# A four-layer graph network: TensorE's fp32 transposes of the activations replaced by two 192 KB DMA transposes per tile

## What is computed

```python
h = relu(layernorm(x));  x = x + gat(relu(gat(h, W1, ...)), W2, ...)
h = relu(layernorm(x));  x = x + gcn(relu(gcn(h, W3, b1)), W4, b2)
# gat: h = x @ W; softmax over each node's incoming edges; weighted sum of h[src]; + bias
# gcn: h = x @ W; sum over incoming edges of h[src] * dinv[src] * dinv[dst]; + bias
```

## Time and profile before

| | |
|---|---|
| median of 3 executions | 2389.45 us (2389.22 to 2395.45) |
| span of the profiled execution | 2395.2 us; the page gives no time of it beside its span, and the slowest of the three is 0.25 us above that |
| TensorE (PE) busy | 2277.9 us, 95% of the span |
| VectorE (DVE), ScalarE (ACT), GpSimd (POOL) busy | 67%, 39%, 39% |
| SP's plain DMAs (q1) | 308.94 MB, 36.7% of the 16 DMA engines' time |
| GpSimd's indirect DMAs (q0) | 172.47 MB, 23.2% of it |
| mean granted TensorE clock | 0.978 of full speed |

### The profile page before, as it was taken

How to read it: one execution, slowest core, us unless ns; L and a number is a source line. 1 busy time by engine, 2 the same in 40 slices (tenths; PEclk the granted TensorE clock), 3 DMA queues, 4 the chain that set the end, 5 groups by cost and what they waited for, 6 DMA issues and landing times.

```text
span 2395.2 us, 45199 instructions
## 1 busy us (share of the span) xinstructions
PE 2277.9 (95%) x14017; PEld 1464.0 (61%) x14017; DVE 1607.5 (67%) x3699; ACT 940.8 (39%) x1271; POOL 933.2 (39%) x1469
## 2 busy tenths in 40 slices
PE   5999999999999999999999999999999999999954
PEld 3666666666666666666566666665666666666621
DVE  5788877775577675443699999655556666668732
ACT  2333343333344454334354445333333434333311
POOL 2333324431534442211366565455433333234354
PEclk9999999999999999999999999999999999999966
DMA  4333332225455554343688888776689988777666
GB/s 167 112 115 116 117 108 98 99 93 184 149 188 192 187 189 151 127 157 118 203 273 288 288 285 276 242 229 216 227 264 308 304 301 303 240 239 258 229 216 203
DMA packets 150732, 482.51 MB, mean 201 GB/s; under 512 B 22265, under 2 KB 22344, under 8 KB 150516
## 3 DMA queue, kind: packets, MB, share of 16 engines
q1 hardware_dynamic: 112804, 308.94, 36.7%
q0 software_dynamic: 37840, 172.47, 23.2%
HBM read 262.87 MB, written 225.76 MB: 204 GB/s over the span
## 4 chain that ended last, share of the span: by engine, by line
PE 68%; DVE 11%; issue 8%; DMA 8%; POOL 4%; ACT 1%; DVEq 0%; POOLq 0%; ACTq 0%
PE ps_h L870 56%; PE ps_z L857 7%; DMA row_in<-in_x,idx_b 4%; DVE bn L1046 2%; DVE pre L1042 2%; DMA edge_mem<-rows,idx_d 2%; DVE pre L1040 2%; PE ps_e L888 1%; DMA out<-base_out,idx_o 1%; PE ps_e L941 1%; PE ps_e L942 1%; DVE edge_mem L1104 1%; POOL rstd L566 1%; POOL edge_mem L551 1%; POOL idx_b L617 1%
## 5 line engine op out<-in xcount | busy, mean ns | idle before, releaser
L870 PE MATMUL ps_h<-w_hi,z_hi 128*128 128x384 f16 x3792 | 929.5, 327 | 0.0
L870 PE MATMUL ps_h<-w_lo,z_hi 128*128 128x384 f16 x3792 | 929.1, 327 | 0.0
L870 PE MATMUL ps_h<-w_hi,z_lo 128*128 128x384 f16 x3792 | 928.7, 327 | 0.0
L1079 DVE TENSOR_TENSOR z_lo<-ps_z,z_hi 128x768 f16<-128x768 f32 x316 | 301.8, 955 | 357.9 <-ACT z_hi L778 354.8
L870 PEld LDWEIGHTS ps_h<-w_lo,z_hi 128*128 128x128 f16 x3792 | 372.0, 98 | 247.2 <-issue 3.0
L870 PEld LDWEIGHTS ps_h<-w_hi,z_lo 128*128 128x128 f16 x3792 | 371.9, 98 | 246.9 <-issue 2.7
L870 PEld LDWEIGHTS ps_h<-w_hi,z_hi 128*128 128x128 f16 x3792 | 372.2, 98 | 219.2 <-issue 15.9
L771 ACT ACTIVATE row_out<-ps_h,grow 128x768 f32<-128x768 f32 x237 | 213.1, 899 | 544.0 <-PE ps_h L870 543.7
L857 PE MATMUL ps_z<-ident,z 128*128 128x128 f32 x1896 | 264.8, 277 | 42.4 <-ACT z L789 35.4
L778 ACT ACTIVATE z_hi<-ps_z 128x768 f16<-128x768 f32 x316 | 254.2, 804 | 46.7 <-PE ps_z L857 46.0
L857 PEld LDWEIGHTS ps_z<-ident,z 128*128 128x128 f32 x1896 | 226.5, 143 | 72.5 <-ACT z L789 40.0
(11 more groups left out here) (213 smaller groups left out, 2324.5 us busy)
## 6 DMA issues: line engine op xcount, KB each, us to landing
rows<-row_out SPq DMA_DIRECT2D x316, 384.0 KB, 3.1
row_in<-rows SPq DMA_DIRECT2D x118, 384.0 KB, 4.2
x_rows<-pre SPq DMA_DIRECT2D x79, 384.0 KB, 4.3
row_in<-x_rows SPq DMA_DIRECT2D x79, 384.0 KB, 4.0
row_in<-in_x SPq DMA_DIRECT2D x78, 384.0 KB, 3.1
rows<-e_out SPq DMA_DIRECT2D x60, 384.0 KB, 3.9
w_raw<-in_L_gnn_W SPq DMA_DIRECT2D x4, 2304.0 KB, 10.0
base_rows<-base_out SPq DMA_DIRECT2D x20, 384.5 KB, 4.3
```

The lines of the kernel that those rows point to most:

```text
L870: last = nc.tensor.matmul(ps_h[s][:, a, 0:HALF], zp[s][:, c, :], wp[:, c, a * HALF:(a + 1) * HALF], start=(c == 0 and zp is z_hi and wp is ...
L1079: V.tensor_tensor(pair3(z_lo[t.slot]), psum_pair(ps_z), pair3(z_hi[t.slot]), ALU.subtract).then_inc(z_lo_ready, 1)
```

## The change

It transposes the activations with the DMA engines in place of TensorE, and splits them before the transposition. ScalarE writes each tile twice from the same input: the upper fp16 part into the left half of `z_half` (128 x 1536 in fp16) and then fp32 `z`. VectorE subtracts the one from the other into the right half. SP issues a transposing DMA for the left half when ScalarE has written it, and another for the right half when VectorE has: 192 KB each, into `z_turn`, 128 x 12 x 128 in fp16 with four buffers. The transposes on TensorE, `ps_z` and the copy of it on ScalarE go. Every step ahead of the products comes one window earlier: ScalarE makes `z(t+3)`, VectorE `low_parts(t+2)` and `prepare(t+4)`, SP turns t+2, loads are for t+5. The weight buffers are two pairs in place of three, and layer 4's weights are dealt with in windows 43 to 53 of `3f`.

```diff
-    t = 0 if phase["before"] else -4
+    t = 0 if phase["before"] else -5
...
-        w_hi = [sb(f"w_hi{s}", [P, KC, D], F16) for s in range(3)]
-        w_lo = [sb(f"w_lo{s}", [P, KC, D], F16) for s in range(3)]
+        w_hi = [sb(f"w_hi{s}", [P, KC, D], F16) for s in range(2)]
+        w_lo = [sb(f"w_lo{s}", [P, KC, D], F16) for s in range(2)]
...
+        z_half = [sb(f"z_half{s}", [P, 2 * D], F16) for s in range(2)]
+        z_turn = [sb(f"z_turn{s}", [P, 2 * KC, P], F16) for s in range(4)]
...
+            def turn(t):
+
+                wait(sp, z_ready, t.g + 1)
+                sp.sem_inc(sp_gate, 1)
+                sp.dma_start_transpose(z_turn[t.slot4][:, 0:KC, :], z_half[t.slot][:, 0:D]).then_inc(z_turned[t.slot4], 16)
+                wait(sp, z_lo_ready, t.g + 1)
+                sp.sem_inc(sp_gate, 1)
+                sp.dma_start_transpose(z_turn[t.slot4][:, KC:2 * KC, :], z_half[t.slot][:, D:2 * D]).then_inc(z_low_turned[t.slot4], 16)
...
             def window(t, side, i, r):
-                if t.exists(4) and t.plus(4).phase["name"] in ("3f", "4f"):
-                    load(t.plus(4))
+                if t.exists(5) and t.plus(5).phase["name"] in ("3f", "4f"):
+                    load(t.plus(5))
                 if t.exists(-1):
                     store(t.plus(-1))
+                if t.exists(2):
+                    turn(t.plus(2))
...
-                    nc.scalar.activation(pair3(z_hi[b.slot]), psum_pair(ps_z), ACT.Copy).then_inc(z_hi_ready, 1)
...
+                if t.exists(3):
+
+                    b = t.plus(3)
                     layer = b.phase["layer"]
-                    wait(act, z_turned, b.g - 1)
+                    wait(act, z_lo_ready, b.g - 1)
+                    if isinstance(b.g, int) and b.g < 2:
+                        pass
+                    else:
+                        act.wait_ge(z_turned[(b.slot4 + 2) % 4], (b.count(b.phase["g0"] - 2, 4) + 1) * 16)
+                        act.wait_ge(z_low_turned[(b.slot4 + 2) % 4], (b.count(b.phase["g0"] - 2, 4) + 1) * 16)
...
+                        nc.scalar.activation(z_half[b.slot][:, 0:D], frm[:, :], ACT.Relu, bias=nmr[b.slot4][:, 0:1],
+                                             scale=rstd[b.slot4][:, 0:1])
                         nc.scalar.activation(z[b.slot][:, :], frm[:, :], ACT.Relu, bias=nmr[b.slot4][:, 0:1],
                                              scale=rstd[b.slot4][:, 0:1]).then_inc(z_ready, 1)
...
-            def turn(t):
-                wait(pe, z_ready, t.g + 1)
-                wait(pe, z_lo_ready, t.g)
-                for c in range(KC):
-                    last = nc.tensor.transpose(ps_z[:, c // 3, (c % 3) * P:(c % 3 + 1) * P],
-                                               z[t.slot][:, c * P:(c + 1) * P], ident[:, :])
-                last.then_inc(z_turned, 1)
...
-                wait(pe, z_lo_ready, t.g + 1)
+                pe.wait_ge(z_turned[t.slot4], (t.slot4_uses + 1) * 16)
+                pe.wait_ge(z_low_turned[t.slot4], (t.slot4_uses + 1) * 16)
...
-                wait(dve, z_hi_ready, t.g + 1)
-                V.tensor_tensor(pair3(z_lo[t.slot]), psum_pair(ps_z), pair3(z_hi[t.slot]), ALU.subtract).then_inc(z_lo_ready, 1)
+                layer, s, s4 = t.phase["layer"], t.slot, t.slot4
+                wait(dve, z_ready, t.g + 1)
+                V.tensor_tensor(z_half[s][:, D:2 * D], z[s][:, :], z_half[s][:, 0:D], ALU.subtract).then_inc(z_lo_ready, 1)
...
-                                                 "2m": {0: lambda: max_w(4), 15: grow4, 16: lambda: low_w(4)}}.get(phase["name"]))
+                                                 "3f": {43: lambda: max_w(4), 52: grow4, 53: lambda: low_w(4)}}.get(phase["name"]))
```

More of the change, by code:

```diff
@@ L88, in phase_uses, with slot4_uses @@
     @property
+    def slot4_uses(self):
+        return self.count(self.phase["g0"], 4)
+    @property
     def phase_uses(self):
@@ L359, in build @@
         z_ready = sem("z_ready")
-        z_turned = sem("z_turned")
-        z_hi_ready = sem("z_hi_ready")
+        z_turned = [sem(f"z_turned{s}") for s in range(4)]
+        z_low_turned = [sem(f"z_low_turned{s}") for s in range(4)]
+        sp_gate = sem("sp_gate")
         z_lo_ready = sem("z_lo_ready")
@@ L573, in window1 @@
                     find_positions(i * 4 + r)
-                if t.exists(3) and t.plus(3).phase["layer"] == 1:
-                    norm_factors(t.plus(3))
-                if t.exists(4) and t.plus(4).phase["layer"] == 2:
-                    load(t.plus(4))
+                if t.exists(4) and t.plus(4).phase["layer"] == 1:
+                    norm_factors(t.plus(4))
+                if t.exists(5) and t.plus(5).phase["layer"] == 2:
+                    load(t.plus(5))
                 if side == "order+mask":
@@ L649, in window @@
             def window(t, side, i, r):
-                if t.exists(4) and t.plus(4).phase["name"] != "4f":
-                    load(t.plus(4))
+                if t.exists(5) and t.plus(5).phase["name"] != "4f":
+                    load(t.plus(5))
                 b = t.plus(-1)
@@ L828, in _ @@
             for phase in chain:
[L829 removed]
+                run_windows(act, phase, window, {"2f": {43: lambda: split_w(3)}, "3f": {52: lambda: split_w(4)}}.get(phase["name"]))
             def last_carry(j, at, per_slot):
@@ L867, in products @@
                 for c in range(KC):
[L868 removed]
+                    for half, wp in ((0, hi), (0, lo), (KC, hi)):
                         for a in range(2):
[L870 to L872 removed]
+                            last = nc.tensor.matmul(ps_h[s][:, a, 0:HALF], z_turn[t.slot4][:, half + c, :], wp[:, c, a * HALF:(a + 1) * HALF],
+                                                    start=(c == 0 and half == 0 and wp is hi),
+                                                    stop=(c == KC - 1 and half == KC))
                     if c == KC - 1:
```

75 lines of the change are left out of this document (31 added, 44 removed).

## The result

The kernel got slower: 2467.12 us median of 4 executions (2458.85 to 2481.51) against 2391.28 of the kernel before (2389.22 to 2395.45), ratio 1.033 [1.029, 1.037]. The forecast was 2443 us. (The two transposing DMAs of a tile are called its pair, and their form the crossbar. SP and SyncE are one engine.)

The account below looks back on a forecast made before the run. TensorE bounds layers 1 and 2; in layers 3 and 4 the DMA engines are near full too. Layers 1 and 2 -103 us, layer 3 +46 and +12, layer 4 +66 and +29, start +4: +54, 2443 us; range 2283 to 2785.

Parts of the forecast that it names:

- its loss of 58 us: Layer 3: DMA time with the pair lengthens windows, +46 us with edges and +12 us in the rest.
- layers 1 and 2 were to bring 103 us: Layers 1 and 2: DMA time stays below TensorE's, so 158 windows each gain the transposes' 0.65 us.
- The pair's price: DMA engines' time for a tile's two transposing transfers: 2.0 us, twice a plain row, between 1.02 and 6.2.
- The rival of the plain price: The pair costs no more than plain bytes, 1.02 to 1.6 us: faster, 2281 to 2375 us; chance 0.35.
- that of the held queue: Transfers hold the queue, 6.2 us a pair, DMA setting every window: much slower, 3640 us; chance 0.12.
- The cap of 0.95: All layers: DMA engines filled to at most 0.95, so DMA time per window was divided by it.
- I cost the wait at nothing: SP's queue: its new wait for VectorE's subtraction delays loads and stores queued behind it at no cost.
- ScalarE's second pass: ScalarE: a Relu pass of at most 1.03 us replaces a 0.80 us copy; 0.23 us more, covered by the window.
- what is late next: ScalarE's wait for both landings of t+1 before writing z_half for t+3: 2 to 3 us of slack in layer 4.
- nothing, or up to 10 us: Layer 3's rest: VectorE's weight maximum and splitting, 4.95 and 5.0 us, covered by work ahead, else up to 10 us.
- the signs for "right": Layers 1, 2: gapless product groups; layers 3, 4: DMA share 0.93 or more, windows 7.2 to 8.8 us, longer landings.
- the signs for "wrong": Layers 3, 4 at 6 to 7 us; layer 2's rest above 7; TensorE awaiting halves at DMA share below 0.8.

Follow-up runs that it names:

- e3: Changed kernel with no transposing DMAs, SyncE only raising the semaphores (nothing moved, transposition left out): 2317.67 us, ratio 0.969.
- e6: Changed kernel with both transposing DMAs issued from ScalarE's queue instead of SyncE's: 2837.44 us, ratio 1.188.
- e4: Changed kernel with each transposing DMA replaced by a plain copy of the same bytes in the same order: 2331.19 us, ratio 0.976.
- e11: As e4, but each half is copied twice, the second time into a spare buffer: 2424.52 us, ratio 1.014.
- e1: Changed kernel with layer 1's row load issued between the two transposing DMAs of a tile: 2443.43 us, ratio 1.024.
- e10: As e9, with layer 1's row load between SyncE's two waits of a tile, as in e1: 2275.70 us, ratio 0.953.
- e9: As e3, with ScalarE writing fp32 z first so the input buffer is freed early: 2293.83 us, ratio 0.961.
- e8: As e1, with ScalarE writing fp32 z first, freeing the input, then waiting for landings and copying into z_half: 2416.12 us, ratio 1.012.
- e2: Changed kernel with four buffers of z_half in place of two: 2471.87 us, ratio 1.034.
- e12: As e10, with the maximum search of layer 4's weights (VectorE's search and GpSimd's reduction) moved back to layer 2: 2264.07 us, ratio 0.947.
- h2: Crossbar in layers 1 and 2 only, TensorE transposing in 3 and 4; row load between halves, input freed early, weights' maximum early: 2319.15 us, ratio 0.970.

## Why the prediction was right or wrong, by its steps

**The direction and the size came out: 2467 for 2443, in the range, on the side that had 0.60.** Of the mechanism a part was right: with the crossbar the DMA engines fill, and layer 4 shows it cleanly, 50 us shorter than before with nothing moved (e3) and 23 longer with the pairs. In layer 3 the step failed. The forecast laid its loss of 58 us to the DMA engines; it lost 53, but 44 of them are there with nothing moved, so they come from the order of the steps and ScalarE's added pass. And the sum is near through errors of opposite sign: layers 1 and 2 were to bring 103 us and brought 16 (or 10, without the shift of a window), while with nothing moved they bring 76; layers 3 and 4 were to cost 153 and cost 76. That part is luck.

**The pair's price: a fifth too low.** The step said 2.0 us between 1.02 and 6.2, as twice a plain row. It is 2.5 (e6's queue). The lower end was right (0.99 in e4 for plain bytes), and the upper was far off: a transfer takes at least 2.7 us from issue to landing, but the pair only 2.5 us of the engines. Put into the forecast's own sum, 2.5 us gives 2539 us, so at the right price it would have been 72 us too high. The rival of the plain price falls, and that of the held queue too. So does the rate behind the plain price: the Trainium skill (DMA: Bandwidth & Descriptors, Latency and other measured facts) gives 261 GB/s and more, and here 393 KB in 2.5 us are 157 GB/s, all engines taken together.

**The cap of 0.95 was no cap.** The forecast divided the sum of DMA times by 0.95 as if a share of 1 were full. The shares reached 1.11. With the measured share and price, layer 4 with edges comes to (6.39 + 2.5) / 1.11 = 8.0 us, the measured window; this only says that the pair's 2.5 us come on top of what was there, as the share is that of the same window. What the highest share is, no run shows. In that stage the plain copies have 1.02 with TensorE full and windows of 6.5 us (e4, 1743 to 1990 us), and 1.02 with windows of 7.7 (e11). At 0.95 and 2.5 it would have been 9.4. Price too low and cap too strict nearly cancelled in layer 4 with edges, and left its rest, forecast at 7.24, at 6.18, below the 6.50 before.

**"I cost the wait at nothing" failed.** The step named all that is queued behind SyncE's new wait, then judged it by layer 3's window, where VectorE subtracts early. In ranking it subtracts behind 7.5 us of rank column (210.57 to 218.11 in the timeline above), and the row load of the next tile but one stands behind. That is worth 24 us in the whole (e1), 40 in layer 1, and 18 in the whole with nothing moved (e10): the largest part of ranking's 7.18 us where 6.19 was forecast. The load's buffer is free once ScalarE has read it, before the subtraction; the load had no need to stand there.

**ScalarE's second pass: covered in its own time, not in what it holds.** The step counted 0.23 us on an engine that is 40% busy. But the two passes, and the wait for the landings ahead of them, now stand before `z_ready`, which frees `row_in` and `pre`. This cost 24 us with nothing moved (e9) and 27 with the crossbar (e8). ScalarE's wait for the landings, "what is late next", is 602 us long, and four buffers took it away without a gain (e2), though that wait, too, stands ahead of the release of the input buffers. So it does not bind; of what e8 and e9 take out of the way, the second pass is what counts.

**The weights: "nothing, or up to 10 us".** The upper bound was the value: 10 us of layer 3, 11.6 of the whole (e12). The step counted VectorE's 4.95 and 5.0 us alone. By e10's trace it was GpSimd's reduction between them, which the sum left out, that TensorE came to wait for.

**What is left open.** With all three mended and nothing moved, layer 3 still takes 591.9 us against 572.6 before, though its transposes are gone. It is not the earlier loads, gathers and stores of kept rows alone: h2 has them, with TensorE's transposes, and takes 572.2. Nor is it layer 3's rest, whose `row_out` come every 6.8 us in both. It lies in the windows with edges, and there TensorE waits 32.4 us for ScalarE's `e_self`, 19 times, which it did for 1.3 us before and 0.8 in h2:

```profile
PE ps_e L944 <- ACT e_self L837: 32.4, 19, 2.4
```

`e_self` stands behind both passes over the tile in ScalarE's order, the second of 0.84 us, and TensorE, without its transposes, has 0.65 us less to do before it. Together that is near the 1.7 us of a wait, but no run moved `e_self`, so it is a reading of the trace. Open too is the second half of layer 1, for which the forecast had no stage: its windows are 7.9 us before, 7.2 with nothing moved and 7.7 with the crossbar, at a DMA share of 0.62 (400 to 530 us).

**What the profile after would show.** Of the signs for "right", layer 2's rest (groups without gap), the DMA share above 0.93 in layers 3 and 4 and windows of 7.2 to 8.8 us came, the last but for layer 4's rest; TensorE's wait on a DMA is there with 76.9 us, 55 of them in layers 3 and 4. But ranking's groups follow with gaps, layer 2 has shares of 0.90 and 1.01 too, and the landings did not lengthen. Layer 3 with edges (1220 to 1500 us) against the earlier trace rows:

```profile
row_in<-rows SPq DMA_DIRECT2D x34, 384.0 KB, 6.3
```

Of the signs for "wrong", the last was a wait of TensorE on the transposed halves at a DMA share below 0.8. It did not come. In ranking, with a share of 0.63, TensorE waits for VectorE's ranking work (the 37.3 us above, 30.3 of them between 70 and 350 us) and not at all for the halves. The order bound there by another way than the sign looked for: through the row load, which holds up VectorE.

## What to carry to other kernels

When a step moves onto a queue, follow for each stage what stands behind its wait, and let everything that doesn't need the step go ahead of it; and look not only at how long an engine is busy with a second pass but at which buffers that pass keeps from being freed. Move work to the DMA engines only in stages where their time per window plus the transfer's stays clear of the window: here the pair cost 13.5 us for its first 1.0 us of DMA time and the next 1.06 us 93, and the crossbar in layers 1 and 2 alone, with the row load ahead, the input freed early and the weights' maximum moved back, made of a loss of 3.3% a gain of 3.0%. A copy of the same bytes in the place of a disputed transfer, once and twice, tells what its bytes and its time on the engines cost; mind that it doubles the issues as well. And run the kernel with nothing moved first: it showed that layer 3's loss, which looked like full DMA engines, was there without them.

## What was unexpected of the hardware

- A transposing DMA of 192 KB from on-chip memory to on-chip memory holds the queue that issues it for 1.21 to 1.24 us at the least, 1.4 us in the median on SyncE and 9.4 us at most (in layer 3, where the DMA share is about 1), where a plain one of 384 KB took 0.35 to 0.42 in ranking.
- It moves in packets of 246 B in the mean (505600 for 316 pairs) and takes 2.5 us of all 16 engines for 384 KB, against 0.99 for the same bytes plain.
- The mean busy share of the DMA engines reached 1.11 over 280 us, at 317 GB/s; a plain mix had 1.02 at 384 GB/s (e11). A share of 1 isn't the end of what this measure shows.
- In layer 3 of the kernels with transposing DMAs, the same code took 625.9 and 650.9 us (changed kernel and e1); with none of them 597.5 and 602.3 (e9, e10), one execution each.
